# First batch of a two-layer transformer kernel: routing gates computed head by head inside the main loop, keys and queries with staging tiles of their own

## The chip, the cores and the metric

The kernel runs on one core of a Trainium2 chip. Its time is the device time of one execution in microseconds (us). The engines of the core are TensorE (PE; its weight loads are listed apart as PEld), VectorE (DVE), ScalarE (ACT), GpSimd (POOL) and SyncE (SP), which here only issues DMAs. Each engine runs its own instructions in the order in which they are written; engines wait for each other on semaphores alone.

## The reference

Input x has B = 4 batches of T = 1024 tokens with D = 128 features. Layer 0, which the change touches, is

```python
xn = layernorm(x)
x = x + multi_query_attention(xn)          # 16 heads of width 8, one key/value head
      + switch_head(xn)                     # 8 heads of width 128, 8 experts each
# switch_head: routing gates for values (gate_v) and for outputs (gate_o)
raw  = sigmoid(xn @ sel_w.T)                # [B, T, 8 heads, 8 experts]
vals, idx = top_k(raw, 2)                   # the two best experts of each head
gate = one_hot(idx) * vals / sum(vals) * route_scale
v    = sum over experts of gate_v * (xn @ v_w[h, e])
ctx  = softmax(q k^T * SCALE) v
out  = sum over experts of gate_o * (ctx @ o_w[h, e])
```

Layer 1 (a linear-feature attention and a routed feed-forward block) follows in the same launch and is not touched.

## The kernel before, in words

Layer 0 is a loop of software-pipelined steps. A step n (0 to 31) is one head h = n % 8 of one batch b = n // 8, of both attentions at once. Loop iteration i (from -2 to 34) on each engine is a list written out by hand: it ends step i, does most of step i + 1 and begins step i + 2. On DVE that is, for step i + 2, `split_queries` (two instructions over 128x1024), `take_peaks` (32 row maxima), `gate_values` (16 products of a PSUM tile with a gate), and for the steps before it `find_largest`, `join_largest`, `lower_ctx`, `output_gates`, `gate_outputs` and `lower_y`. TensorE writes all results but the sums into a ring of 7 PSUM tiles; a tile is claimed again when DVE or ACT has emptied it, in the order of claims.

Between these calls stand eight places, `batch_work(i, 0)` to `batch_work(i, 7)`, where work for another batch is slipped in. On DVE, place 0 stands before `join_largest(i + 1, 2)` and `split_queries(i + 2)`; place 1 between `split_queries` and `lower_ctx(i, 3)`; place 2 between `gate_values(i + 2, 1, 0)` and `(1, 1)`; place 3 within the peaks of tile row 4; place 4 before `gate_values(i + 2, 4, 1)`; place 5 before `lower_y(i + 2, 0)`; place 6 between `gate_values(i + 2, 5, 0)` and `(5, 1)`; place 7 before the last four peaks. In them batches 1 to 3 get their gates: iterations with i % 8 from 1 to 5 compute the gates of the batch after, one instruction or a few at each place.

Gates for four token tiles are made by `gates(b, part)`, 17 parts with 21 DVE instructions, each waiting for the one before it (`Chain`). Fifteen of them run over 128x512 elements, the others over 128x128 or 128x64. A batch takes two such passes.

Batch 0 has no loop to hide in; it is prepared ahead of the loop:

- SP loads x, 13 constants, the first weights, the rest of x, then stores zeros to two DRAM buffers `q_dram` (L747, L748), then stores the queries of each half (`store_queries`, three DMAs each, L669), then loads the queries of head 0 (`load_queries(0)`, four DMAs, L681), which waits until all stores have landed.
- PE turns xn, then computes `logits` (L419), then for each half `keys` (L427) and `queries` (L435), then `qk_products`.
- ACT waits for the constants, takes the root of the variance, keeps xnT, then `upper_x`, `upper_wv`, the four `sigmoid_exps`, then for each half `keep_keys` and `keep_queries`. Keys and queries of both halves go through one staging tile, `kf`, so each write waits until DVE (`lower_keys`) or the store's DMAs have read what was there.
- DVE takes the four `keep_v32`, `lower_keys(0, 0)`, the first pass of gates, `lower_keys(0, 1)`, `lower_qk`, the second pass of gates, and enters the loop with `split_queries(0)`.
- POOL lowers x (L87), adds a bias (L793) and lowers the first value weights (L87).

These lines are the preparation on DVE:

```python
for l in range(4):
    keep_v32(0, l)
lower_keys(0, 0)
for part in range(17):
    gates(0, part)
lower_keys(0, 1)
lower_qk()
for part in range(17, 34):
    gates(0, part)
```

Of the kernel before, what the change touches and what calls it, by code (L numbers as in the profile page):

```python
# [16 lines left out]
P = 128  # L17
# [162 lines left out]
def layer0(nc, whole, a, x, xnT, ident, order, combine, choice, xn_dram, listed, xs, spare, wvs, w):  # L180
# [4 lines left out]
    with ExitStack() as ctx:  # L185
# [15 lines left out]
        xo = oT[:, :].rearrange("p (t d) -> p t d", t=TPB)  # L201
        lg = m.sbuf("lg", [P, TPB, EM])
# [17 lines left out]
        probT = [m.sbuf(f"probT{k}", [P, TPB, 2 * P]) for k in range(2)]  # L220
        ctxT = [m.sbuf(f"ctxT{k}", [PS, 2, 2 * P]) for k in range(2)]
# [33 lines left out]
        steps, batches = range(N0), range(B)  # L255

# [9 lines left out]
        with nc.Block() as block:  # L266
            @block.tensor
            def _(pe):
# [378 lines left out]
            def _(sp):  # L647
# [13 lines left out]
                def store_queries(b, q):  # L661
# [5 lines left out]
                    for part in range(3):  # L667
                        rows = slice(2 + part * HD, 2 + (part + 1) * HD)
                        sp.dma_start(q_dram[b % 2][:, rows, q * 512:(q + 1) * 512], kf[:, :]).then_inc(q_stored, 16)  # L669
# [61 lines left out]
                def load_layer1():  # L731
                    sp.wait_ge(xn_turned, 2 * B)
                    sp.wait_ge(gates_ready, 2 * B)
# [158 lines left out]
            def _(act):  # L892
# [38 lines left out]
                def keep_turned(n, t, h):  # L931
# [95 lines left out]
                def keep_keys(b, q):  # L1027
# [7 lines left out]
                    if b or q:  # L1035
                        act.wait_ge(ks_ready, 2 * b + q)
                        act.wait_ge(q_stored, 64 + (96 * b if b else 48 * q))
                    act.activation(kf[:, :], ring.home["keys", b, q][:, :], ACT.Identity, bias=bk[:, :]).then_inc(k_kept, 1)

                def keep_queries(b, q):  # L1040
# [5 lines left out]
                    act.wait_ge(ks_ready, 2 * (b + 1) if b else q + 1)  # L1046
                    if b or q:
                        act.wait_ge(q_stored, 64 + 48 * (2 * b + q))
                    act.activation(kf[:, :], ring.home["queries", b, q][:, :], ACT.Identity, bias=bq[:, :], scale=HD ** -0.5)\
# [52 lines left out]
                keep_qk()  # L1102
# [89 lines left out]
            def _(v):  # L1192
# [20 lines left out]
                def gate_values(n, t, c):  # L1213
# [3 lines left out]
                    if t == 0 and c == 0:  # L1217
                        v.wait_ge(gates_ready, 2 * (n // HS + 1))
# [87 lines left out]
                ln, gs, mx = Chain(v, ln_step), Chain(v, gate_step), Chain(v, mix_step)  # L1306
# [47 lines left out]
                def lower_keys(b, q):  # L1354
                    if b not in batches:
# [3 lines left out]
                    v.scalar_tensor_tensor(out=kq.bitcast(F32R), in0=kq, scalar=split[:, 1:2], in1=kf[:, :],  # L1359
                                           op0=ALU.mult, op1=ALU.add).then_inc(ks_ready, 1)  # L1360

                def gates(b, part):
# [4 lines left out]
                    ranks = order[:, :].unsqueeze(1).to_broadcast([P, 64, ES])  # L1367
                    if part == 0:
                        v.wait_ge(gates_exp, 4 * b + 2 * q + 2)
                        gs(v.scalar_tensor_tensor(out=g_v[:, :, :], in0=flat, scalar=1.0, in1=flat, op0=ALU.add, op1=ALU.max))  # L1370
                    if part == 1:
                        gs(v.tensor_reduce(g_pair[:, 0, :], g_v[:, :, :], AX.X, ALU.min))
                    if part == 2:
                        gs(v.tensor_tensor(g_c[:, :, :], g_v[:, :, :], spread(g_pair[:, 0, :], ES), ALU.is_equal))
                    if part in (3, 9):
                        gs(v.tensor_tensor(g_c[:, :, :], g_c[:, :, :], ranks, ALU.mult))
# [1320 lines left out]
```

## Time and profile before

| | |
|---|---|
| time, median of 3 (lowest to highest) | 3180.81 us (3178.78 to 3181.18) |
| the profiled execution, its own time | 3167.05 us |
| its span, first to last instruction | 3165.2 us |
| mean granted TensorE clock | 0.969 |
| PE busy | 2945.3 us (93%) |
| DVE busy | 2427.8 us (77%) |
| POOL busy | 1846.8 us (58%) |
| ACT busy | 1619.2 us (51%) |

Busy times are sums over one execution. A step of the loop takes about 75 to 80 us; the preparation and the first two iterations take longer than the steady steps and use TensorE little. Durations below are those of the profiled execution, which is 13.8 us shorter than the median of the three runs.

### The profile page before, as it was taken

How to read it: one execution, taken by the hardware profiler on the slowest of the kernel's cores; microseconds unless marked ns; L12 is line 12 of the kernel's file. 1: busy time of each engine (PE TensorE's matmuls, PEld its weight loads, DVE VectorE, ACT ScalarE, POOL GpSimd, SP SyncE). 2: the span in 40 equal slices, each digit the busy share in tenths (PEclk: the TensorE clock that was granted, in tenths of full speed). 3: DMA queues.
4: the chain of work that ended last, by engine and by line, in shares of the span. 5: the costliest groups of instructions: out<-in, count | busy, mean ns of one | idle time of the engine just before them, and what ended most of it. 6: DMA issues, size and time to landing. Idle time of an engine off the chain costs nothing. (4 is left out here: it accounts for less than half of the span.)

```text
span 3165.2 us, 51840 instructions
## 1 busy us (share of the span) xinstructions
PE 2945.3 (93%) x17486; PEld 2054.4 (65%) x17486; DVE 2427.8 (77%) x4551; ACT 1619.2 (51%) x3277; POOL 1846.8 (58%) x2277
## 2 busy tenths in 40 slices
PE   4999999999999999999999999999999965798997
PEld 2666666666676666666666666666676643466674
DVE  7788898888889988898898988888888652245343
ACT  1455555555555555555555555555555621444634
POOL 2556666666676666666666676666666535334330
PEclk7999999999999999999999999999999978899998
DMA  5000001100100110101001100010010021133222
GB/s 168 21 22 22 22 22 32 32 22 23 37 27 22 32 32 22 29 23 36 29 22 32 32 22 23 22 43 28 22 39 22 10 43 45 56 89 110 84 76 85
DMA packets 139849, 124.63 MB, mean 39 GB/s; under 512 B 28410, under 2 KB 122116, under 8 KB 139492
## 3 DMA queue, kind: packets, MB, share of 16 engines
q1 hardware_dynamic: 125892, 88.46, 10.0%
q0 software_dynamic: 10160, 30.17, 3.0%
q10 hardware_dynamic: 3536, 2.69, 0.5%
q8 instruction: 143, 2.34, 0.3%
q14 instruction: 118, 0.97, 0.1%
HBM read 97.49 MB, written 29.30 MB: 40 GB/s over the span
## 5 line engine op out<-in xcount | busy, mean ns | idle before, releaser
L849 POOL TENSOR_TENSOR m_vprod<-m_vprod 128x512 f32<-128x512 f32 x256 | 336.1, 1313 | 721.4 <-DVE m_vprod L1223 721.4
L1210 DVE TENSOR_REDUCE m_peaks<-m_ring 128x1 f32<-128x512 f32 x1024 | 643.4, 682 | 23.9 <-PE m_ring L293 22.7
L957 ACT ACTIVATE m_expA<-m_ring 128x512 f32<-128x512 f32 x1024 | 543.9, 605 | 162.4 <-PE m_ring L366 159.2
L928 ACT ACTIVATE m_prob<-m_ring,m_negs 128x512 f32<-128x512 f32 x512 | 347.4, 684 | 404.4 <-DVE m_negs L1261 403.6
L344 PE MATMUL m_ring<-m_probT,m_vs 128*128 128x256 f32 x2048 | 473.8, 384 | 11.7 <-DVE m_oprod L1294 10.2
L344 PEld LDWEIGHTS m_ring<-m_probT,m_vs 128*128 128x128 f32 x2048 | 379.9, 190 | 83.8 <-issue 35.1
L1294 DVE TENSOR_TENSOR m_oprod<-m_ring,m_go 128x512 f32<-128x512 f32 x512 | 347.4, 685 | 73.5 <-POOL k_x L862 44.8
L1223 DVE TENSOR_TENSOR m_vprod<-m_ring,m_gate 128x512 f32<-128x512 f32 x512 | 348.8, 685 | 68.2 <-PE m_ring L99 41.0
L1251 DVE TENSOR_REDUCE m_negs<-m_ring 128x1 f32<-128x512 f32 x512 | 346.0, 685 | 39.2 <-PE m_ring L99 37.0
L858 POOL TENSOR_TENSOR m_oprod<-m_oprod 128x512 f32<-128x512 f32 x256 | 327.9, 1281 | 70.6 <-DVE m_oprod L1294 70.4
L938 ACT ACTIVATE m_probT<-m_ring 128x512 f32<-128x512 f32 x512 | 301.0, 605 | 103.9 <-PE m_ring L332 98.3
L332 PE MATMUL m_ring<-k_ident,m_prob 128*128 128x128 f32 x2048 | 309.6, 276 | 0.5 <-ACT m_probT L938 0.4
L332 PEld LDWEIGHTS m_ring<-k_ident,m_prob 128*128 128x128 f32 x2048 | 242.8, 141 | 76.0 <-issue 31.6
L381 PE MATMUL m_sums<-m_expA,m_v 128*32 128x512 f32 x2048 | 273.6, 606 | 0.6 <-ACT m_expA L957 0.5
L97 PE MATMUL m_ring<-k_wvs,k_xs 128*128 128x512 f32 (+1 forms) x536 | 234.3, 437 | 14.7 <-POOL k_wvs L87 7.0
L97 PE MATMUL m_ring<-k_xs,m_yT 128*128 128x512 f32 x512 | 219.8, 429 | 2.5 <-DVE m_oprod L1294 2.1
L97 PE MATMUL m_ring<-m_wos,m_ctxT 128*128 128x512 f32 x512 | 213.0, 416 | 1.0
L99 PE MATMUL m_ring<-k_wvs,k_xs 128*128 128x512 f32 (+1 forms) x536 | 212.3, 396 | 0.0
L98 PE MATMUL m_ring<-k_wvs,k_xs 128*128 128x512 f32 (+1 forms) x536 | 211.6, 395 | 0.0
L98 PE MATMUL m_ring<-m_wos,m_ctxT 128*128 128x512 f32 x512 | 202.9, 396 | 0.0
L99 PE MATMUL m_ring<-k_xs,m_yT 128*128 128x512 f32 x512 | 202.7, 396 | 0.0
L850 POOL TENSOR_TENSOR m_vprod<-m_vprod 128x256 f32<-128x256 f32 x256 | 190.8, 745 | 20.1
(311 smaller groups left out, 5396.9 us busy)
## 6 DMA issues: line engine op xcount, KB each, us to landing
m_wraw<-in_v_w SPq DMA_DIRECT2D x32, 512.0 KB, 4.0
m_qf<-q_dram SPq DMA_DIRECT2D x128, 128.0 KB, 2.7
m_wraw<-in_o_w SPq DMA_DIRECT2D x32, 512.0 KB, 4.0
q_dram<-m_kf SPq DMA_DIRECT2D x24, 256.0 KB, 3.0
listed<-in_pad SPq DMA_DIRECT2D x6, 897.0 KB, 12.2
m_xg<-listed SPq DMA_DIRECT2D x39, 138.0 KB
m_rows<-answers SPq DMA_DIRECT2D x8, 512.0 KB, 4.0
sums_dram<-m_sumsT ACTq DMA_DIRECT2D x128, 18.0 KB
```

What stands on the lines that cost most here:

```text
L97: pe.matmul(out, wh, xh, start=True, stop=False)
L98: pe.matmul(out, wh, xl, start=False, stop=False)
L99: return pe.matmul(out, wl, xh, start=False, stop=True)
L332: last = pe.transpose(ps[:, c * P:(c + 1) * P], prob[t % 2][:, (4 * h + c) * P:(4 * h + c + 1) * P], ident[:, :])
L344: last = pe.matmul(ps[:, 0:2 * P], vs[n % 2][:, k, :], probT[g % 2][:, k, :], start=(k == 0), stop=(k == TPB - 1))
L849: vchain(pool.tensor_tensor(vprod[:, 0:512], vprod[:, 0:512], vprod[:, 512:1024], ALU.add))
L928: act.activation(prob[t % 2][:, c * 512:(c + 1) * 512], ring.home["scores", n, t, c][:, :], ACT.Exp, bias=neg[t % 2], accum_out=den[n % 2] ...
L957: act.activation(expA[hh][:, c * 512:(c + 1) * 512], ring.home["scT", n, k, hh, c][:, :], ACT.Exp)\
L1210: v.tensor_reduce(peaks[:, t, hh, c:c + 1], ring.home["peaks", n, t, hh, c][:, :], AX.X, ALU.max)\
L1223: v.tensor_tensor(vprod[:, c * 512:(c + 1) * 512].rearrange("p (e d) -> p e d", e=4), ring.home["values", n, t, c][:, :].rearrange("p (e d ...
L1251: v.tensor_reduce(half_neg[:, t % 2, c:c + 1], ring.home["scores", n, t, c][:, :], AX.X, ALU.max, negate=True)\
L1294: v.tensor_tensor(oprod[t % 2][:, c * 512:(c + 1) * 512].rearrange("p (e d) -> p e d", e=4), ring.home["outputs", n, t, c][:, :].rearrange ...
```

## The change

The gates of batch 0 are made by `first_gates(h, part)`: one head at a time, for all eight token tiles, with the same 21 instructions in 17 parts as before, now over 128x128 elements (16 groups of 8 experts) where they ran over 128x512. Head 0 is done ahead of the loop. Head i + 3 is done in iteration i, so heads 1 to 7 in iterations -2 to 4: two parts at each of the places 0 to 6 and three at place 7. The scratch tiles lie in `oT`, which is first used later. All four exponentials of batch 0 are awaited before the first part.

The keys and queries of batch 0 get four staging areas in `probT[0]`, so the waits between them fall away; the first `keep_turned` takes up the wait for `ks_ready` and `q_stored` instead. PE and ACT do keys and queries before the logits; ACT takes the root before it waits for the constants, and does `upper_x` and `upper_wv` after the exponentials; DVE does both `lower_keys` first. No DMA is added, removed or moved in its queue.

```diff
+        h_v, h_one, h_c, h_other = (oT[:, k * P:(k + 1) * P].rearrange("p (g e) -> p g e", e=ES) for k in range(4))
+        h_pair, h_inv = (oT[:, k:k + 4 * TPB].rearrange("p (k g) -> p k g", k=2) for k in (4 * P, 4 * P + 4 * TPB))
+        h_m = oT[:, 4 * P + 8 * TPB:4 * P + 10 * TPB]
+        first_kf = probT[0][:, :, :].rearrange("p t q -> p (t q)").rearrange("p (w q d) -> p w q d", w=2, q=2)
+        def kf_of(b, what, q):
+            return kf[:, :] if b else first_kf[:, what, q, :]
...
# PE
-                for l in range(4):
-                    logits(0, l)
                 for q in range(2):
                     keys(0, q)
                     queries(0, q)
+                for l in range(4):
+                    logits(0, l)
...
# ACT, keep_turned
+                    elif g == 0 and t == 0 and h == 0:
+                        act.wait_ge(ks_ready, 2)
+                        act.wait_ge(q_stored, 64 + 96)
# ACT, keep_keys and keep_queries: the waits on ks_ready and q_stored only if b > 0, kf_of(b, ...) for kf
...
+                roots(1, slice(0, TPB))
                 act.wait_ge(consts_loaded, 16 * n_consts)
-                roots(1, slice(0, TPB))
                 keep_xnT(0, 0)
                 keep_xnT(0, 1)
-                upper_x(0)
-                upper_wv(0, ahead=True)
-                for l in range(4):
-                    sigmoid_exps(0, l)
                 for q in range(2):
                     keep_keys(0, q)
                     keep_queries(0, q)
+                for l in range(4):
+                    sigmoid_exps(0, l)
+                upper_x(0)
+                upper_wv(0, ahead=True)
                 keep_qk()
...
# DVE, gate_values
-                    if t == 0 and c == 0:
-                        v.wait_ge(gates_ready, 2 * (n // HS + 1))
# DVE: gate_part(chain, part, flat, tiles, n) holds the 21 instructions for both gates() and
+                def first_gates(h, part):
+                    if not 0 <= h < HS:
+                        return
+                    flat = gate_of[0][:, :, :].rearrange("p t (k g e) -> p (t k) g e", k=2, e=ES)[:, :, h, :]
+                    if part == 0:
+                        v.wait_ge(gates_exp, 4)
+                    gate_part(gs, part, flat, (h_v, h_one, h_c, h_other, h_m, h_pair, h_inv), 2 * TPB)
+                    if part == 16:
+                        gates_kept(v.tensor_tensor(flat, h_one, h_other, ALU.add))
...
                 def batch_work(i, place):
+                    for part in range(2 * place, 2 * place + 2 + place // 7):
+                        first_gates(i + 3, part)
                     if i not in steps:
                         return
...
+                lower_keys(0, 0)
+                lower_keys(0, 1)
                 for l in range(4):
                     keep_v32(0, l)
-                lower_keys(0, 0)
                 for part in range(17):
-                    gates(0, part)
-                lower_keys(0, 1)
+                    first_gates(0, part)
                 lower_qk()
-                for part in range(17, 34):
-                    gates(0, part)
```

## Rows read from the trace of the kernel before

**Rows 1.** The page, busy time of each engine: us, share of the span, instructions.
```profile
PE 2945.3 (93%) x17486; PEld 2054.4 (65%) x17486; DVE 2427.8 (77%) x4551; ACT 1619.2 (51%) x3277; POOL 1846.8 (58%) x2277
```

**Rows 2.** Timeline of the preparation: start, us, engine, line, tiles, [idle before <-releaser].
```profile
10.03 0.21 ACT L980 ACTIVATE m_rstd<-m_va 128x8 f32<-128x8 f32 x1 [1.33 <-DMA m_bq<-in_bq]
...
14.22 4.30 PE L419 MATMUL m_ring<-m_selv,k_xnT 128*128 128x160 f32 x16
...
18.76 0.85 SPq L748 DMA_DIRECT2D q_dram<-m_vprod  x1
...
19.21 1.02 PE L435 MATMUL m_ring<-k_xnT,m_wq 128*128 128x512 f32 x2
...
22.61 17.17 SPq L669 DMA_DIRECT2D q_dram<-m_kf  x6
...
27.01 0.69 ACT L1038 ACTIVATE m_kf<-m_ring,m_bk 128x512 f32<-128x512 f32 x1 [3.85 <-DMA q_dram<-m_kf]
...
37.27 0.69 ACT L1049 ACTIVATE m_kf<-m_ring,m_bq 128x512 f32<-128x512 f32 x1 [9.57 <-DVE m_ks L1359]
...
42.21 1.75 SPq L681 DMA_DIRECT2D m_qf<-q_dram  x4
...
55.16 0.80 PE L293 MATMUL m_ring<-m_ks,m_qs 32*128 32x512 f32 x4 [31.42 <-DVE m_qs L1202]
```

**Rows 3.** Timeline of DVE, instructions of the two passes of gates.
```profile
21.71 1.22 DVE L1370 SCALAR_TENSOR_TENSOR k_spare<-m_gate 128x512 f32<-128x512 f32 x1
...
39.68 0.68 DVE L1370 SCALAR_TENSOR_TENSOR k_spare<-m_gate 128x512 f32<-128x512 f32 x1
...
48.36 0.95 DVE L1391 RECIPROCAL m_g_inv<-m_g_pair 128x128 f32<-128x128 f32 x1
49.34 0.23 DVE L1392 TENSOR_TENSOR m_g_m<-m_g_inv 128x64 f32<-128x64 f32 x1
...
50.71 0.29 DVE L1398 TENSOR_TENSOR m_g_inv<-m_g_inv,m_g_m 128x128 f32<-128x128 f32 x1
```

**Rows 4.** Timeline of POOL, the first value weights lowered.
```profile
21.32 4.01 POOL L87 TENSOR_TENSOR k_wvs<-m_wraw,k_wvs 128x256 fp32r<-128x256 f32 x4
```

**Rows 5.** The page's DMA issues: count, KB each, us from issue to landing.
```profile
m_qf<-q_dram SPq DMA_DIRECT2D x128, 128.0 KB, 2.7
```

**Rows 6.** Waits of DVE from 55.1 to 95.6 us (iteration -2): total us, times, longest.
```profile
DVE m_vprod L1223 <- POOL m_vs L851: 8.2, 4, 2.8
```

**Rows 7.** Windows, one per step, iterations -1 to 6 and 15: length, busy us (x), PEclk, DMA share, GB/s.
```profile
95.64:166.97 71.33, 68.06 (x362) 46.23 (x363) 57.03 (x107) 39.37 (x85) 36.10 (x46) 0.95 0.08 23
166.97:255.85 88.88, 81.79 (x424) 55.45 (x422) 77.61 (x171) 45.53 (x94) 48.98 (x66) 0.94 0.07 19
255.85:333.53 77.68, 76.17 (x423) 52.94 (x422) 66.12 (x123) 44.90 (x94) 52.52 (x66) 1.00 0.08 22
333.53:410.99 77.46, 76.69 (x425) 53.12 (x424) 69.73 (x125) 43.43 (x93) 52.18 (x65) 1.00 0.08 22
410.99:488.76 77.77, 76.89 (x419) 52.44 (x418) 70.78 (x127) 43.39 (x92) 52.20 (x66) 1.00 0.08 23
488.76:565.13 76.37, 75.58 (x417) 52.03 (x416) 68.12 (x122) 43.10 (x91) 51.62 (x65) 1.00 0.12 33
565.13:641.19 76.06, 75.12 (x416) 51.82 (x414) 68.99 (x125) 41.64 (x89) 52.90 (x65) 1.00 0.12 33
641.19:715.79 74.60, 73.97 (x416) 51.32 (x414) 62.36 (x114) 41.67 (x89) 49.64 (x65) 1.00 0.09 23
...
1327.35:1401.99 74.64, 74.01 (x416) 51.36 (x414) 67.40 (x130) 41.67 (x89) 49.73 (x65) 1.00 0.08 24
```

**Rows 8.** Windows, one stretch around the turn from iteration 2 to 3.
```profile
400.95:424.96 24.01, 23.59 (x133) 17.36 (x134) 23.40 (x43) 15.48 (x34) 18.28 (x23) 1.00 0.07 23
```

**Rows 9.** Lines of DVE from 255.85 to 641.19 us: xcount, busy us, mean ns.
```profile
L1387 DVE TENSOR_TENSOR k_spare<-k_spare,m_g_pair 128x512 f32<-128x512 f32 x2 | 2.5, 1270 | 0.0
...
L1374 DVE TENSOR_TENSOR k_spare<-k_spare,m_g_pair 128x512 f32<-128x512 f32 x2 | 1.8, 894 | 0.0
```

More of the change, by code:

```diff
@@ L1034, in keep_keys @@
                                    ACT.Identity, bias=bk[:, :])
-                    if b or q:
+                    if b:
                         act.wait_ge(ks_ready, 2 * b + q)
-                        act.wait_ge(q_stored, 64 + (96 * b if b else 48 * q))
-                    act.activation(kf[:, :], ring.home["keys", b, q][:, :], ACT.Identity, bias=bk[:, :]).then_inc(k_kept, 1)
+                        act.wait_ge(q_stored, 64 + 96 * b)
+                    act.activation(kf_of(b, 0, q), ring.home["keys", b, q][:, :], ACT.Identity, bias=bk[:, :]).then_inc(k_kept, 1)
                 def keep_queries(b, q):
@@ L1045, in keep_queries @@
                     act.wait_ge(q_made, 2 * b + q + 1)
-                    act.wait_ge(ks_ready, 2 * (b + 1) if b else q + 1)
-                    if b or q:
+                    if b:
+                        act.wait_ge(ks_ready, 2 * (b + 1))
                         act.wait_ge(q_stored, 64 + 48 * (2 * b + q))
-                    act.activation(kf[:, :], ring.home["queries", b, q][:, :], ACT.Identity, bias=bq[:, :], scale=HD ** -0.5)\
+                    act.activation(kf_of(b, 1, q), ring.home["queries", b, q][:, :], ACT.Identity, bias=bq[:, :], scale=HD ** -0.5)\
                         .then_inc(q_kept, 1)
@@ L1358, in lower_keys, with gate_part @@
                     v.wait_ge(k_kept, 2 * b + q + 1)
-                    v.scalar_tensor_tensor(out=kq.bitcast(F32R), in0=kq, scalar=split[:, 1:2], in1=kf[:, :],
+                    v.scalar_tensor_tensor(out=kq.bitcast(F32R), in0=kq, scalar=split[:, 1:2], in1=kf_of(b, 0, q),
                                            op0=ALU.mult, op1=ALU.add).then_inc(ks_ready, 1)
+                def gate_part(chain, part, flat, tiles, n):
+                    vals, one, c, other, mo, pair, inv = tiles
+                    ranks = order[:, :].unsqueeze(1).to_broadcast([P, n, ES])
+                    if part == 0:
+                        chain(v.scalar_tensor_tensor(out=vals, in0=flat, scalar=1.0, in1=flat, op0=ALU.add, op1=ALU.max))
+                    if part == 1:
+                        chain(v.tensor_reduce(pair[:, 0, :], vals, AX.X, ALU.min))
+                    if part == 2:
+                        chain(v.tensor_tensor(c, vals, spread(pair[:, 0, :], ES), ALU.is_equal))
+                    if part in (3, 9):
+                        chain(v.tensor_tensor(c, c, ranks, ALU.mult))
+                    if part in (4, 10):
+                        chain(v.tensor_reduce(mo, c, AX.X, ALU.max))
+                    if part == 5:
+                        chain(v.tensor_tensor(one, c, spread(mo, ES), ALU.is_equal))
+                    if part == 6:
+                        chain(v.scalar_tensor_tensor(out=vals, in0=one, scalar=3.0e38, in1=vals, op0=ALU.mult, op1=ALU.add))
+                    if part == 7:
+                        chain(v.tensor_reduce(pair[:, 1, :], vals, AX.X, ALU.min))
+                    if part == 8:
+                        chain(v.tensor_tensor(c, vals, spread(pair[:, 1, :], ES), ALU.is_equal))
+                    if part == 11:
+                        chain(v.tensor_tensor(other, c, spread(mo, ES), ALU.is_equal))
+                    if part == 12:
+                        chain(v.reciprocal(inv, pair))
+                        chain(v.tensor_tensor(mo, inv[:, 0, :], inv[:, 1, :], ALU.add))
+                    if part == 13:
+                        chain(v.tensor_tensor(mo, mo, tiny[:, :].to_broadcast([P, n]), ALU.max))
+                        chain(v.reciprocal(mo, mo))
+                        chain(v.tensor_tensor(mo, mo, route[:, :].to_broadcast([P, n]), ALU.mult))
+                    if part == 14:
+                        chain(v.tensor_tensor(inv, inv, mo.unsqueeze(1).to_broadcast([P, 2, n]), ALU.mult))
+                    if part == 15:
+                        v.tensor_tensor(one, one, spread(inv[:, 0, :], ES), ALU.mult)
+                        chain(v.tensor_tensor(other, other, spread(inv[:, 1, :], ES), ALU.mult))
```

45 lines of the change are left out of this document (6 added, 39 removed).

## The prediction

> **What bounds the kernel now.** I read the page first, then the windows by step, then the timeline of the preparation engine by engine. The page shows TensorE busy for 93% of the span [rows 1]; a change in DVE work pays or costs only where TensorE waits for it. The windows show where that is. In a step with little extra work (iteration 6) TensorE is busy 73.97 of 74.60 us while DVE has 12.2 us to spare; in iterations 2 to 4 DVE's spare time is down to 7.7, 7.0 and 8.3 us [rows 7]. The timeline of the preparation shows the opposite: the first matmul of the loop starts at 55.16 us after TensorE has stood idle for 31.42 us, released by `split_queries` on DVE (L1202) [rows 2]. There DVE is what counts. Behind it lies a chain through one staging tile: ACT waited 3.85 us for the stores of the first queries, then 9.57 us for `lower_keys(0, 1)`, which stood behind the first pass of gates; only then could the second half be stored (loads issued at 42.21 us), and the second pass of gates held DVE until 53 us anyway [rows 2].
>
> So the change takes DVE work from a place where all of it is on the path, and puts most of it, in smaller pieces, into steps that are bound by TensorE but have DVE nearly full.
>
> **What one head costs on DVE.** An instruction over 512 elements takes 0.68 us, over 128 elements 0.29, over 64 elements 0.23; a reciprocal over 128 takes 0.95 [rows 3]. From one start to the next it is some 0.035 us more. Of the 21 instructions of a head 15 run over 128 elements: 15 x 0.325 = 4.9 us. The reciprocals over 32 and 16 elements and the four others come to an estimated 1.5 us. A head alone is 6.4 us, eight heads 51 us. The two passes before took 14.7 and 13.4 us (21.7 to 36.4, 39.7 to 53.1), 28 us. The change adds 23 us of DVE work, because the fixed part of an instruction is paid four times as often.
>
> The Trainium skill speaks against this edit (VectorE: DVE Perf Modes, section on the TRN2 errata): a fixed latency is paid per instruction, so tiles should have 512 elements or more. The rows above agree, a quarter of the elements costs 0.29 of 0.68 us; by elements alone the eight heads would cost 28 us.
>
> POOL adds to this. With POOL lowering weights from 21.32 on [rows 4], the first gate instruction took 1.22 us, the same one later 0.68 [rows 3]; in iterations 1 to 5 the same kind averaged 0.89 and 1.27 us on two lines [rows 9]. So an instruction with two SBUF operands waits 0 to 0.6 us for POOL. I take 0.26, near the lower of the two lines, for the 12 large instructions of that kind: 3.1 us, 9.5 us for a head in the loop. That this wait is as long for a short instruction as for a long one is my choice; if it goes by length it is 1.2 us, if there is none a head is 6.4.
> The Trainium skill would choose the same (SBUF — State Buffer, section on the two sides of SBUF): it calls the port pair of VectorE and GpSimd an exclusive lock held for a whole instruction.
>
> **The preparation, step by step.** (1) The root no longer waits for the last constant: 1.33 us less [rows 2]. (2) xnT is complete at 13.7 us; four matmuls of keys and queries, at 0.86 us each, end at 16.3, the logits (4.3 us for all) at 20.5 [rows 2]. (3) ACT's six evictions end at 17.6; table load, exponentials after the last logits: 21.4. (4) Stores: SP has issued the zero fills by 19.61 [rows 2]; nothing of this moves. Six stores at 0.6 us are issued by 23.3. Before, three issued at 22.61 had landed at 27.0, and the other three took 4.2 us from 38.0 to 42.21 [rows 2]. All six landed: 25.7 (23.3 + 2.4) to 31.2 (27.0 + 4.2); I take 28.8, one more trio of data behind the first. (5) The four loads issue over 1.75 us, the last 1.3 after the first, and land 2.7 later [rows 2, 5]: 32.9, between 29.7 and 35.2. (6) DVE: gates of head 0 from 21.4, 6.4 + 3.1 us beside POOL, to 30.9; `lower_qk` 1.3; place 0 of iteration -2 0.7: 32.9. Both arrive together. `split_queries` takes 2.0: first peak matmul at 35.0 instead of 55.16, **20 us earlier** (17 to 22). POOL's lowering moves from 25.3 to 31.4 at the latest, still before the first values. ACT's `upper_x` and `upper_wv` stand before `keep_qk`, hidden behind the gates. The new wait in `keep_turned` holds ACT's queue for nothing: keys and stores are 50 us old then. The dropped wait of `gate_values` and the one at the end of a head cost nothing, DVE's own order covers them. SP's wait in `load_layer1` counts the same event.
>
> **What is given back in the loop.**
> - Iteration -2 is a chain of DVE and POOL: DVE waits 8.2 us for POOL in four waits [rows 6]. The parts at places 2, 3, 4 and 6 lie on it (0.65 each) and the three at place 7 (1.15); place 5 falls in a wait, place 1 in the wait for the first peaks. 3.75 us, with POOL's waits 4.3 (up to 5.5).
> - Iterations -1 to 4 get 9.5 us each. Two bounds. *Saturation:* iterations 6 and 15 differ by 5.0 us of DVE work and not in length, iteration 5 has 6.6 more than 6 and is 1.46 longer [rows 7]; as if DVE could be busy 90% for nothing and each us beyond cost 0.9. *Filling:* the 24 us around the turn from iteration 2 to 3 had DVE busy 23.40 us and TensorE 23.59 [rows 8], so DVE can be full without stopping TensorE; then only what does not fit beside 2 us of idle time counts.
> - Iterations 2, 3, 4: filling 69.7 + 9.5 + 2 - 77.5 = 3.7, likewise 4.5 and 3.2, sum 11.4; saturation 3 x 8.5 = 25.6. Iteration 1: 0 or 5.0. Iteration 0: 0.2 or 6.2. Iteration -1: 0.65 (place 0 stands before a `split_queries` that TensorE awaits) or 1.9 [rows 7].
> - Sum with iteration -2: 16.0 (with 3.75) by filling, 44 by saturation. I take a third of the way, **25.5 us**, since the stretch of rows 8 is direct evidence and the parts are small and spread.
>
> What is late next: a late DVE empties ring tiles late, and TensorE stops at a claim. From iteration 7 on nothing differs.
>
> **Sum.** -20 + 25.5 = +5.5 us: 3172.6 us for an execution like the profiled one (3167.05), 3186.3 against the median of the runs, which stands 13.8 us above that execution.
>
> **Rivals.**
> - *Filling, B.* -20 + 16 = -4: 3176.8 us. For it: rows 8. Against it: no step in rows 7 shows DVE above 91% with gates in it.
> - *The steps swallow it, D, the other side.* Short instructions don't wait for POOL, a head costs 6.4 us and the idle time of the steps takes it: filling gives 0.6 + 1.4 + 0.1 = 2.1 in iterations 2 to 4, 0.65 and 3.75 before: 6.5 in all, -13.5: 3167.3 us. It decides if the loop gives back less than 12.6 us. For it: iterations 6 and 15.
> - *Saturation, C.* Each us on DVE is paid: -20 + 44 = +24: 3204.8. For it: iterations 3 and 5. It may bring the clock down as in iterations -1 and 0 (0.95 and 0.94) [rows 7].
> - *A short preparation gain, E.* Each of the 12 instructions of head 0 waits 0.54 us for POOL as the first one did (1.22 against 0.68), or loads land at 35.2: 17 us gained, 3189.3. The lock rule of the Trainium skill (SBUF — State Buffer, the section on the two sides) works this way: whoever comes second waits for the whole instruction. The trace agrees for the first instruction and leaves the short ones open.
> - That the change does not do what it says is excluded by the order of the queues: nothing else holds the second stores.
>
> **Chances.** Forecast A 0.35 (its own range 3180 to 3193), B 0.25, D 0.18, C 0.14, E 0.08. Below 0.2% (6.4 us) a difference can't be told from none here. Faster: D and a fifth of B, 0.23. Slower: C, most of E, over half of A, 0.39. The rest 0.38. The forecast stands at the edge of "slower"; what is likely is a small number either way. Range: from between D and B, 3171, to just short of C, 3200.
>
> **What would show it.** In the profile after: first L293 matmul at 34 to 38 us, released by L1202; the DMA loads of m_qf issued at 27 to 31 us; no idle of 9 us on ACT; `cut_peaks(0)` (L1233, at 93.25 before) 15 to 16 us earlier; iterations 2 to 4 longer by 3 to 8 us each with DVE above 95% busy; the 128x128 gate instructions at 0.29 us alone and with a mean of 0.5 beside POOL; from iteration 7 on the same lengths. The prediction is wrong if these iterations keep their length (then D), or if the queries land after 35 us.

## The result

The changed kernel takes 3206.46 us (median of 4, 3202.74 to 3208.58) where the kernel before, run beside it, takes 3179.80 (4 runs, 3175.00 to 3181.18): ratio 1.0102, interval 1.0083 to 1.0122. It is 1% slower; the two medians by themselves are 26.7 us apart. The forecast was 3186.3 with a range of 3171 to 3200, so the prediction was wrong. The rival *Saturation*, 3204.8, came nearest.

The profiled execution took 3206.8 us (span 3205.0, mean granted clock 0.965), 39.8 us more than the profiled one of before. At the start of iteration 30, the last mark that is compared here, it is 35.3 us behind (2512.72 and 2477.39). The other 4.4 us lie behind that mark, nearly all of it layer 1. That rest varied between the profiled executions of all kernels here: 654 to 661 us in the four that were taken on one chip, 688 to 705 in the ten others, with no order by kernel. So the traces are compared up to that mark, and times by the ratios of one comparison.

**The page**, busy time of each engine [rows 1]:

```profile
PE 2973.6 (93%) x17486; PEld 2070.6 (65%) x17486; DVE 2473.6 (77%) x4677; ACT 1619.9 (51%) x3277; POOL 1849.0 (58%) x2277
```

DVE has 126 instructions and 45.8 us more. PE has 28.3 us more busy time for the same instructions; why is told with the clock, below.

**The preparation**, from the timelines of the changed kernel [rows 2]:

```profile
16.32 0.71 ACT L1060 ACTIVATE m_probT<-m_ring,m_bq 128x512 f32<-128x512 f32 x1
17.04 1.28 ACT L1034 ACT_TABLE_LOAD   x1
...
19.58 0.29 DVE L1376 SCALAR_TENSOR_TENSOR m_oT<-m_gate 128x128 f32<-128x128 f32 x1 [1.16 <-ACT m_gate L1034]
...
19.97 5.26 SPq L677 DMA_DIRECT2D q_dram<-m_probT  x6
...
21.20 2.00 DVE L1386 TENSOR_TENSOR m_oT<-m_oT 128x128 f32<-128x128 f32 x1
...
28.07 1.75 SPq L689 DMA_DIRECT2D m_qf<-q_dram  x4
...
32.21 0.69 DVE L83 CAST m_qs<-m_qf 128x1024 fp32r<-128x1024 f32 x1 [0.16 <-DMA m_qf<-q_dram]
...
34.28 0.80 PE L301 MATMUL m_ring<-m_ks,m_qs 32*128 32x512 f32 x4 [14.34 <-DVE m_qs L1213]
```

The first peak matmul starts at 34.28 us instead of 55.16: 20.9 us earlier, 20 were forecast. The chain is the one forecast. The queries are kept at 17.0, the six stores follow without the long waits of before, the loads go out at 28.07, and DVE waits for them 0.16 us only, since its gates of head 0 end at 30.2. One of those, 0.29 us long by itself, was held for 2.00 us while POOL lowered x.

**The loop**, one window for each iteration from -2 to 6 [rows 7]. The first window begins with the first peak matmul, each later one where TensorE starts the transposes of `qf` for the next head. Columns are length, busy us (x) of PE, PEld, DVE, ACT, POOL, then PEclk, DMA share, GB/s:

```profile
34.28:80.61 46.33, 36.12 (x93) 20.41 (x93) 38.69 (x71) 1.19 (x2) 16.89 (x21) 0.68 0.29 101
80.61:155.76 75.15, 68.80 (x361) 46.55 (x362) 66.21 (x128) 39.41 (x85) 37.02 (x47) 0.95 0.08 22
155.76:252.49 96.73, 83.38 (x424) 56.36 (x423) 83.78 (x192) 45.56 (x94) 49.51 (x66) 0.93 0.06 18
252.49:338.77 86.28, 80.66 (x423) 54.93 (x422) 75.57 (x144) 45.09 (x94) 52.75 (x66) 0.96 0.07 20
338.77:425.20 86.43, 81.95 (x425) 56.10 (x424) 78.75 (x146) 43.44 (x93) 51.73 (x65) 0.96 0.07 20
425.20:511.62 86.42, 82.05 (x419) 55.31 (x418) 79.20 (x148) 43.59 (x92) 52.05 (x66) 0.96 0.07 20
511.62:598.01 86.39, 80.19 (x418) 54.63 (x416) 77.59 (x143) 43.06 (x91) 51.26 (x65) 0.96 0.10 29
598.01:674.84 76.83, 75.69 (x415) 52.00 (x414) 69.67 (x125) 41.60 (x89) 52.32 (x64) 1.00 0.11 33
674.84:749.49 74.65, 73.94 (x416) 51.35 (x415) 62.40 (x114) 41.67 (x89) 49.77 (x65) 1.00 0.09 23
```

Set against rows 7 (iteration -2 of before is the 40.48 us from 55.16 to 95.64, with DVE busy 31.40), all in us:

| iteration | longer by | forecast (filling / saturation) | DVE busy, added | DVE idle, before | DVE idle, after |
|---|---|---|---|---|---|
| -2 | 5.9 | 3.75 to 5.5 | 7.3 | 9.1 | 7.6 |
| -1 | 3.8 | 0.65 / 1.9 | 9.2 | 14.3 | 8.9 |
| 0 | 7.9 | 0.2 / 6.2 | 6.2 | 11.3 | 13.0 |
| 1 | 8.6 | 0 / 5.0 | 9.5 | 11.6 | 10.7 |
| 2 | 9.0 | 3.7 / 8.5 | 9.0 | 7.7 | 7.7 |
| 3 | 8.7 | 4.5 / 8.5 | 8.4 | 7.0 | 7.2 |
| 4 | 10.0 | 3.2 / 8.5 | 9.5 | 8.3 | 8.8 |

Look at the last two columns. In iterations 2 to 4 DVE is given 9 us of work and has about as much idle time as before: in sum, none of it was filled. The seven iterations give back 53.8 us; 25.5 were forecast and 44 was the upper bound. Iteration 5 adds 0.8; nearly all later ones agree to some tenths. -20.9 + 53.8 is +32.9; iteration 5 and small differences of the 24 later ones make it the 35.3 us at the mark.

**What DVE waits for.** Its longer waits in iteration 3 (total us, times, longest), before:

```profile
DVE m_ctxT L87 <- ACT m_ctxT L948: 2.0, 3, 1.3
DVE m_oprod L1294 <- POOL k_x L862: 1.4, 1, 1.4
```

and in the changed kernel:

```profile
DVE m_vprod L1232 <- PE m_ring L99: 1.6, 3, 0.6
DVE m_oprod L1303 <- POOL k_x L870: 1.4, 1, 1.4
DVE m_negs L1260 <- PE m_ring L99: 1.4, 3, 0.7
```

The wait for ACT shrank from 2.0 to 0.4 us, so the new work did fill that one. The waits for TensorE grew from 2.2 us in all to 4.0, and the one for POOL stayed at 1.4. The rows read as an exchange: DVE comes late, TensorE stops, and later DVE waits for what TensorE has not made. Iteration 1 shows the same, 4.7 to 1.7 us for ACT and 4.9 to 6.8 for TensorE.

**What TensorE sees.** Four neighbouring windows in iteration 3 of the changed kernel:

```profile
432.11:435.57 3.46, 3.40 (x18) 2.77 (x16) 3.35 (x6) 2.75 (x7) 3.30 (x4) 1.00 0.00 0
435.57:439.02 3.45, 1.95 (x15) 0.58 (x15) 3.31 (x6) 2.05 (x4) 2.74 (x4) 1.00 0.01 2
439.02:442.48 3.46, 3.45 (x9) 2.22 (x10) 2.85 (x5) 1.09 (x2) 0.00 (x0) 0.58 0.54 152
442.48:445.94 3.46, 3.46 (x17) 2.78 (x16) 2.40 (x5) 1.09 (x2) 1.96 (x2) 0.92 0.00 0
```

DVE is full (3.31 of 3.45) and TensorE stands idle for 1.5 us; 0.6 us after it works again, its granted clock goes to the lower of its two levels, 1.2 GHz of 2.4, for 3.4 us. The waits of PE in this iteration name the places:

```profile
PE m_ring L374 <- DVE m_ctxT L87: 1.5, 1, 1.5
PE m_ring L374 <- ACT m_prob L936: 1.1, 1, 1.1
PE m_ring L301 <- DVE m_oprod L1303: 0.7, 1, 0.7
```

Before, the longest wait of this iteration was 0.4 us and its clock was 1.00. Now each of iterations 1 to 4 spends 8% of its length at half clock (PEclk 0.96): 0.04 x 86.4 = 3.5 us of full-clock time is lost in each, 14 of the 19.5 us by which PE's busy time grows in these four. Whether that makes the iterations longer is a question of its own, and kernels 10 and 11 ask it.

### The profile page after: what moved, and what is told of

It is laid out like the page before. It is cut to its first block and busy times, and to the rows that moved or that the text cites. A ratio compares the mean times of both kernels' runs of the same rounds, so it can differ in the third digit from the quotient of the medians.

```text
span 3205.0 us, 51986 instructions
## 1 busy us (share of the span) xinstructions
PE 2973.6 (93%) x17486; PEld 2070.6 (65%) x17486; DVE 2473.6 (77%) x4677; ACT 1619.9 (51%) x3277; POOL 1849.0 (58%) x2277
## 5 line engine op out<-in xcount | busy, mean ns | idle before, releaser
L352 PE MATMUL m_ring<-m_probT,m_vs 128*128 128x256 f32 x2048 | 475.5, 385 | 12.2 <-DVE m_oprod L1303 10.6
L97 PE MATMUL m_ring<-k_wvs,k_xs 128*128 128x512 f32 (+1 forms) x536 | 236.8, 442 | 13.0 <-POOL k_wvs L87 6.0
L99 PE MATMUL m_ring<-k_wvs,k_xs 128*128 128x512 f32 (+1 forms) x536 | 215.1, 401 | 0.0
L98 PE MATMUL m_ring<-k_wvs,k_xs 128*128 128x512 f32 (+1 forms) x536 | 214.4, 400 | 0.0
L374 PEld LDWEIGHTS m_ring<-m_qs,m_ks 32*128 32x128 f32 x1024 | 64.0, 182 | 229.7 <-issue 119.5
```

What stands on the lines that cost most here:

```text
L97: pe.matmul(out, wh, xh, start=True, stop=False)
L98: pe.matmul(out, wh, xl, start=False, stop=False)
L99: return pe.matmul(out, wl, xh, start=False, stop=True)
L352: last = pe.matmul(ps[:, 0:2 * P], vs[n % 2][:, k, :], probT[g % 2][:, k, :], start=(k == 0), stop=(k == TPB - 1))
```

## The experiments

Every kernel of a comparison ran on one chip beside the kernel before. In the first comparison that one took 3133.83 us, in the others 3181.37, 3181.76 and 3181.21: chips differ by more than the change, so only ratios are used. An unchanged copy, profiled on the chip of the first comparison, agrees with the first profile of before within 1.6 us at the start of iteration 30.

**1. The preparation alone.** Heads 1 to 7 get no gates:

```diff
                 def batch_work(i, place):
-                    for part in range(2 * place, 2 * place + 2 + place // 7):
-                        first_gates(i + 3, part)
```

> The changed kernel with the gates of heads 1 to 7 of batch 0 left out altogether (their exponentials are used as gates), so only the preparation is changed. All theories: the first peak matmul of the loop at 34.3 us as in the changed kernel (55.2 before), and all iterations as long as before. Time 3159 us, ratio 0.9935 (21 us less). If the ratio is above 0.997, the early start is lost again later without any gate work, and the loop is not where the loss lies.

Measured: ratio 0.9942 (0.9921 to 0.9963), some 18 us less (15 by the medians alone); at the start of iteration 30 it is 21 us ahead of the unchanged copy on the same chip. The first peak matmul starts at 34.40 us and every iteration keeps its length of before (40.46, 71.24, 88.71, 77.66, 77.59, 77.75, 76.38). The gain ahead of the loop is real and lasts, and what the changed kernel loses it loses to the pieces in the loop.

**2. The same number of instructions, half of them without a second SBUF operand.** 10 of the 21 instructions of heads 1 to 7 become row maxima over the same 128x128 elements, so these heads get no valid gates:

```diff
                 def first_gates(h, part):
...
+                    if h and part in (2, 3, 5, 6, 8, 9, 11, 15, 16):
+                        for k in range(1 + (part == 15)):
+                            (gates_kept if part == 16 else gs)(v.tensor_reduce(h_m, h_v, AX.X, ALU.max))
+                        return
```

> The changed kernel, but for heads 1 to 7 ten of the 21 instructions, those over 128x128 with two SBUF operands, are row maxima over the same 128x128 elements instead (0.28 us each, one operand; the gates of these heads are not made). The number of instructions stays. Theory saturation by busy time: DVE work falls by what was waited for POOL, about 3 us a head, and so does each step: iterations 1 to 4 go from 86.4 to 83 us, time about 3188, ratio 1.002. Theory that number and place of the instructions count and not their length: no change, 3205. Theory filling: with 6.3 us a head the work fits in, iterations 1 to 4 at 79 us, time 3173.

Measured: ratio 1.0038 (1.0024 to 1.0052). In iterations 1 to 4 DVE's busy time grows by 6.3, 5.7, 4.9 and 6.3 us and the lengths by 6.2, 4.7, 4.1 and 6.0. Iteration 3:

```profile
412.62:494.45 81.83, 78.04 (x419) 52.81 (x418) 75.68 (x148) 43.60 (x92) 51.66 (x66) 1.00 0.08 22
```

The same number of instructions gives back 21.0 us in these iterations instead of 36.2: it is their time on DVE that counts. DVE idles 6.2 us of iteration 3.

**3. Where the pieces stand.** All 17 parts at places 2 to 7, none at the turn from one iteration to the next (before `split_queries` and `lower_ctx`):

```diff
-                    for part in range(2 * place, 2 * place + 2 + place // 7):
-                        first_gates(i + 3, part)
+                    if place >= 2:
+                        for part in range(3 * place - 6, min(3 * place - 3, 17)):
+                            first_gates(i + 3, part)
```

> The changed kernel with the same 21 instructions per head, but none at places 0 and 1 (before split_queries and lower_ctx): three parts at each of places 2 to 6, two at place 7. Theory saturation: the same DVE work in the same iteration, the same time, 3206 us, ratio 1.008 to 1.012. Theory turn: TensorE stops at the turn of an iteration because split_queries and lower_ctx come late, and its clock falls to half after it; with places 0 and 1 free iterations 1 to 4 fall from 86.4 to 81 us or less with the clock at 1.00, time 3185 or less, ratio 1.002.

Measured: ratio 1.0083 (1.0060 to 1.0106); iterations 1 to 4 at 84.8, 83.2, 84.3 and 82.7 us with 8.4, 7.3, 7.1 and 8.3 us more on DVE. They give back 25.8 us instead of 36.2, and half of that difference is that the same instructions waited less for POOL (31.1 us of DVE time added instead of 36.4). The place is worth some 5 us in these four; as the main cause the turn is ruled out. Iteration 4 is 6.4 us longer here though its clock stays at 1.00.

**4 and 5. DVE work that nobody needs, put into the kernel before**, where the gates of batch 0 don't disturb: 16 instructions over 128x128 in each of iterations 5 to 9, two at each place. In the fourth kernel they are row maxima, in the fifth products of two SBUF tiles:

```diff
+                    for _ in range(2 if 5 <= i <= 9 else 0):
+                        extra(v.tensor_reduce(ex_m, ex_a, AX.X, ALU.max))         # 4
+                        extra(v.tensor_tensor(ex_b, ex_b, ex_a, ALU.mult))        # 5, instead
```

> The kernel before (gates of batch 0 ahead of the loop as before), with extra work alone: in iterations 5 to 9 two row maxima over 128x128 elements, each waiting for the one before, at each of the eight places: 16 x 0.31 = 5.0 us more DVE work per iteration, one operand each, nothing waits for them. Before, these iterations have DVE busy 69.0, 62.4, 66.2, 63.6 and 65.6 us and last 76.1, 74.6, 74.6, 75.5 and 76.0. Theory ceiling at 90 to 91% busy: iteration 6 (67.4 of 74.6) keeps its length, 7 (71.2) becomes 78.5, 8 and 9 (68.6, 70.6) 75.5 and 78, iteration 5 (74.0) 81.5. Theory that every us costs from the first on: all five 4 to 5 us longer. Theory filling: none longer by over 0.5 us but iteration 5.

> As the run with extra row maxima, but the 80 extra instructions multiply two SBUF tiles of 128x128 elements. Alone such an instruction takes 0.29 us too. Theory that the wait for POOL does not depend on the length of the instruction: a mean of 0.55 us or more, single ones above 1.5 us, DVE busy some 4 us more per iteration than with the row maxima, and iterations longer by about 0.9 of that. Theory that the wait goes by length, as 1.06 to 0.69 for 512 elements: a mean of 0.35 us and iterations as long as with the row maxima within 1 us.

Measured, one run each: 3186.08 and 3199.48 us, beside 3181.37 of before. Lines of DVE over the two kernels, first 4, then 5:

```profile
L1496 DVE TENSOR_REDUCE m_oT<-m_oT 128x16 f32<-128x128 f32 x80 | 22.4, 280 | 1.4
```

```profile
L1496 DVE TENSOR_TENSOR m_oT<-m_oT 128x128 f32<-128x128 f32 x80 | 46.6, 582 | 1.4
```

A product that takes 0.29 us alone [rows 3] takes 0.58 in the loop, a row maximum 0.28: the second operand costs 0.29 us on average. It is the wait for POOL: the 28 products that started while POOL was idle took 0.28 us on average and never over 0.30, the 52 that started while POOL was busy 0.74. The price of DVE time (us):

| iteration | DVE idle before | 4: DVE added, longer by | idle left | 5: DVE added, longer by | idle left |
|---|---|---|---|---|---|
| 5 | 7.1 | 4.7, 3.8 | 6.1 | 8.2, 7.8 | 6.7 |
| 6 | 12.2 | 3.7, 0.3 | 8.9 | 8.8, 1.4 | 4.9 |
| 7 | 8.4 | 4.2, 2.4 | 6.7 | 7.7, 4.3 | 5.0 |
| 8 | 11.9 | 3.6, 0.2 | 8.5 | 8.2, 1.8 | 5.5 |
| 9 | 10.4 | 5.7, 1.1 | 5.8 | 9.0, 4.2 | 5.6 |

Here the threshold is seen directly. Between 8 and 9 us cost 1.4 us in iteration 6, which had 12.2 us to spare, and 7.8 in iteration 5, which had 7.1. Whatever an iteration had, 5 to 7 us of DVE's idle time are left when it is full. Iterations 5 and 6 of the fifth kernel:

```profile
567.10:650.97 83.87, 79.61 (x416) 54.05 (x415) 77.16 (x143) 41.66 (x89) 52.74 (x65) 0.98 0.10 30
650.97:726.95 75.98, 75.41 (x415) 51.90 (x414) 71.13 (x130) 41.82 (x89) 49.96 (x65) 1.00 0.08 23
```

**6. The new staging and order with both wide passes ahead**, nothing in the loop:

```diff
-                for part in range(17):
-                    first_gates(0, part)
+                for part in range(34):
+                    gates(0, part)
```

> The changed preparation (staging tiles, order, root), but both passes of gates over 128x512 elements are made ahead of the loop as in the kernel before, and none in the loop. Theory that the start is bound by DVE once the staging waits are gone: gates from 19.6 us, 28 us of them and 3 us of waits for POOL, lower_qk 1.3, split_queries 2: first peak matmul at 53 to 55 us against 55.2, ratio 0.999 to 1.000. Theory that the staging chain was the bound and gates were in its shadow: 40 us, ratio 0.995.

Measured: ratio 0.9998 (0.9989 to 1.0007). The first peak matmul starts at 53.57 us. The new staging and order alone are worth 1.6 us: with the chain of stores gone, the 28 us of gates on DVE set the start.

**7. Fewer iterations, wider instructions**, the gates complete: head 0 ahead, head 1 in iteration -2, heads 2 and 3 at once (256 wide) in -1, heads 4 to 7 at once (512 wide) over iterations 0 and 1:

```diff
+                    if i < -1:
+                        todo, heads = range(2 * place, 2 * place + 2 + place // 7), slice(1, 2)
+                    elif i < 0:
+                        todo, heads = range(2 * place, 2 * place + 2 + place // 7), slice(2, 4)
+                    elif i < 2:
+                        todo, heads = range(8 * i + place, 8 * i + place + 1 + i * (place // 7)), slice(4, 8)
...
```

> The same gates complete, but the heads are taken in wider instructions: head 0 ahead, head 1 in iteration -2, heads 2 and 3 by one 256-wide pass in iteration -1, heads 4 to 7 by one 512-wide pass over iterations 0 and 1, nothing in iterations 2 to 4. Ceiling theory: the DVE time beyond the free 4 us is paid in iterations 0 and 1 alone: -20.9 us ahead, +5.5 in iteration -2, +5 to 6 in -1, +7 to 8 in each of 0 and 1: +5 to +6 us in all, ratio 1.001 to 1.003, iterations 2 to 4 at their 77.5 us again. Per-instruction theory (each two-operand instruction beside POOL costs the same wait, so that the number of instructions and not their length decides): iterations 0 and 1 cost 4 us or less each, total -3 us or better, ratio 0.999 or less.

Measured: ratio 1.0012 (1.0002 to 1.0022). Iterations -2 to 1 are longer by 5.9, 5.4, 4.6 and 9.2 us, iterations 2 to 4 as before, which is what the ceiling gives in sum (the split between 0 and 1 was expected even). But iterations 0 and 1 paid 4.6 us for 5.3 us of DVE time and 9.2 for 9.4, though each had over 11 us idle before: next to nothing was free there. A price by the instruction is ruled out: 13 more of them in iteration 1 cost 9.2 us, as much as 21 short ones did, because they are longer.

**8. Pieces only where DVE has room**, the gates complete: heads 0 and 1 ahead (256 wide), heads 2 to 7 in one pass 768 wide over iterations -2 and -1:

```diff
+                    at = {-2: (0, 0, 1, 2, 3, 4, 5, 6, 7), -1: (7, 7, 7, 9, 11, 13, 14, 15, 17)}.get(i)
+                    for part in range(*at[place:place + 2]) if at else ():
+                        first_gates(slice(2, 8), part)
...
-                    first_gates(0, part)
+                    first_gates(slice(0, 2), part)
```

> The changed preparation with gates of heads 0 and 1 ahead in one pass over 128x256 elements, and heads 2 to 7 in one pass over 128x768 elements in iterations -2 and -1 (none at place 0): 42 instructions instead of 168, and none in iterations 0 to 4, where DVE is near its ceiling. Theory ceiling: first matmul at 37 to 38 us, iteration -2 longer by 5 to 6, iteration -1 by 4 to 6, all others as before: 5 to 8 us less than before, ratio 0.9975 to 0.9985. If work in iterations -2 and -1 costs in full (22 us), ratio 1.001.

Measured: 3171.33 us against 3181.37, ratio 0.9969 (0.9957 to 0.9982): faster than both kernels. Iterations -2 to 1:

```profile
36.17:81.63 45.46, 36.47 (x92) 20.58 (x92) 37.91 (x59) 1.19 (x2) 17.40 (x21) 0.68 0.25 81
81.63:158.74 77.11, 70.54 (x361) 47.45 (x362) 69.49 (x121) 39.14 (x85) 38.45 (x47) 0.96 0.07 21
...
248.23:325.94 77.71, 76.20 (x424) 52.95 (x422) 66.17 (x123) 44.90 (x94) 52.57 (x66) 1.00 0.08 22
```

It gives back 5.0 and 5.8 us in the first two iterations, where DVE had 9.1 us of 40 and 14.3 of 71 idle and was given 6.5 and 12.5. Iteration 0 is 0.6 us longer, as it is by 0.4 in the unchanged copy, and nothing is given back after it.

**9. Edits 2 and 3 together** (heads 1 to 7 again without valid gates).

> The changed kernel with both earlier edits at once: of the gate instructions of heads 1 to 7, 10 of 21 are one-operand row maxima (so heads 1 to 7 get no valid gates), and the pieces stand at places 2 to 7 of an iteration alone. Ceiling theory (an iteration of about 77.7 us has some 4 us of DVE time to fill, and each us of DVE work beyond costs 0.8 to 1.0 us): DVE is given about 5 to 5.5 us in each of iterations 1 to 4, one more is saved by the places, so they come to 79 to 81 us instead of 86.4, layer 0 ends about 5 to 8 us earlier than with the one-operand edit alone, and the ratio to the kernel before is 0.999 to 1.002. Turn theory (work in the places beside the cores' turns is what costs): as the gates are off the turns already in the earlier run, the one-operand form adds little, iterations 82 to 84 us, ratio 1.005 or more.

Measured: ratio 1.0045 (1.0032 to 1.0058), between the two expectations. Iterations 1 to 4 are longer by 3.3, 3.9, 4.3 and 5.9 us for 6.7, 5.3, 5.1 and 6.3 us on DVE, so 0.5 to 0.9 us for each; iteration 0 is 96.07, 2.9 us longer than in kernel 2. The ceiling holds (idle left: 8.2, 6.3, 6.2, 7.9 us), but which places cost more than others in iteration 0 isn't settled.

**10 and 11. Is it the clock?** The changed kernel (10) and the kernel before (11) get six more 128x512 matmuls, overwritten at once, at each of six points of iterations 1 to 4. Four of the points, in iterations 2 and 3, stand where the changed kernel had a gap and then half clock. The one in iteration 1 comes at 268.14 us, when the clock has already fallen, and the one in iteration 4 fills a gap after which the clock had not fallen.

```diff
                 def scores_by_key(n, k, hh, c):
...
+                    if hh == 0 and c == 0 and (k, n) in ((0, 2), (0, 3), (0, 4), (6, 3), (6, 4), (6, 5)):
+                        for _ in range(2):
+                            matmul3(pe, ps[:, :], both(xs[b % 2], slice(0, P)), both(xs[b % 2], slice(0, 512)))
```

> The changed kernel, and TensorE does six more 128x512 matmuls (1.4 us at full clock, overwritten at once) at six points where it stood idle for 1.1 to 1.5 us and its granted clock then fell to half: before the scores of key tile 0 in steps 2, 3, 4 and of key tile 6 in steps 3, 4, 5. Clock theory (a full DVE makes gaps, the gaps bring the clock down, and the half clock costs 1.7 us at each fall, 3.4 us in each of iterations 1 to 4): the granted clock of these iterations goes from 0.96 to 0.98 or 1.00, and each is 1.5 to 3.4 us shorter, in all 6 to 12 us less than the changed kernel, ratio to the kernel before 1.006 to 1.008. Rival (DVE sets the length, the slow TensorE only uses up time in which it would wait): the clock may recover, but the iterations keep 86 to 87 us and the ratio 1.010. If the fillers themselves delay: 88 us.

> The kernel before with the same six groups of extra matmuls: the price of a filler where TensorE has no gap to fill. Both theories: 1.4 us each where nothing is idle, some 6 to 8 us in all, iterations 1 to 4 at 79 to 80.5 us with the clock at 1.00, ratio 1.002 to 1.003.

Measured: ratios 1.0110 (1.0092 to 1.0128) and 1.0029 (1.0016 to 1.0042). In kernel 11 iterations 1 to 4 are 79.20, 79.28, 79.00 and 77.62 us, 5.5 us more than in the unchanged copy for some 8.2 us of matmuls. In kernel 10 they are 88.76, 86.50, 87.98 and 86.87: 4.6 us more than in the changed kernel. Their clock is 0.94, 0.98, 0.96 and 0.96, so it rose in iteration 2 only, where the clock theory had 0.98 to 1.00 in all four; the rival's 86 to 87 us and 1.010 came nearer. Iteration 2 is the one to read. Timeline of PE in kernel 10 where the first filler stands (its weights are `k_xs` alone), and later, at the end of this iteration:

```profile
355.92 0.40 PE L99 MATMUL m_ring<-k_xs 128*128 128x512 f32 x1
356.25 0.72 PE L377 MATMUL m_ring<-m_qs,m_ks 32*128 32x512 f32 x4
...
357.48 0.40 PE L98 MATMUL m_ring<-k_wvs,k_xs 128*128 128x512 f32 x1
...
412.90 0.50 PE L301 MATMUL m_ring<-m_ks,m_qs 32*128 32x512 f32 x1
415.80 0.75 PE L301 MATMUL m_ring<-m_ks,m_qs 32*128 32x512 f32 x3 [2.40 <-DVE m_oprod L1306]
```

and the same places in the changed kernel:

```profile
353.34 1.00 PE L374 MATMUL m_ring<-m_qs,m_ks 32*128 32x512 f32 x3 [0.84 <-DVE m_ctxT L87]
...
355.10 0.63 PE L98 MATMUL m_ring<-k_wvs,k_xs 128*128 128x512 f32 x1
...
413.37 0.49 PE L301 MATMUL m_ring<-m_ks,m_qs 32*128 32x512 f32 x1
414.58 0.50 PE L301 MATMUL m_ring<-m_ks,m_qs 32*128 32x512 f32 x3 [0.72 <-DVE m_oprod L1303]
```

Here the filler does what it should: with the gap filled the next matmuls run at full clock, 0.40 us each where the changed kernel needs 0.63. So at this place the clock's fall hangs on the gap. A gap isn't always followed by one: after 2.61 us of idle time at 325.57 us the clock of the changed kernel stayed at 1.00. Counted from the start of the iteration (341.45 and 338.77), L301 is reached at 71.45 us instead of 74.60, over 3 us ahead. Then TensorE stands still for 2.40 us instead of 0.72, because DVE, which ran without a pause for 13 us up to there, had not come to `gate_outputs` (L1306). Just ahead of that product DVE had five gate instructions in a row, four of them of the first batch. Two of these, and the product:

```profile
412.00 1.36 DVE L1408 TENSOR_TENSOR m_oT<-m_oT 128x128 f32<-128x128 f32 x1
...
413.60 0.69 DVE L1431 TENSOR_TENSOR m_gate<-m_oT 128x128 f32<-128x128 f32 x1
...
415.05 0.69 DVE L1306 TENSOR_TENSOR m_oprod<-m_ring,m_go 128x512 f32<-128x512 f32 x1
```

The clock falls there instead, and the iteration ends at 86.50 us, as in the changed kernel at 86.43. Iteration 3 repeats it: its wait of 0.7 us at L301 becomes 2.4. In both, what the clock gave was taken back by the wait for DVE. Nor is a fall of the clock needed for the loss: the six iterations of kernels 2, 3 and 9 among 1 to 4 whose clock stayed at 1.00 are 3.3 to 6.4 us longer, 0.5 to 0.84 us for each us on DVE. The changed kernel paid 0.9 to 1.06. Part of that difference may be the clock's, which no run here shows. How much shorter the iteration would be with the clock held at full throughout can't be read from these runs, since the fillers cost time themselves.

## Why the prediction was wrong

**Right: the preparation.** 20.9 us for 20, by the forecast steps: loads issued at 28.07 (27 to 31 was said), no idle time of 9 us on ACT, start at 34.28 (34 to 38), released by `split_queries`. `cut_peaks(0)` came 15.0 us earlier (15 to 16). Two terms were off and nearly cancel, which is luck: head 0 took 10.6 us (19.6 to 30.2) where 9.5 was said, as one instruction took 2.00 and one 1.23 us beside POOL; and it began at 19.6 instead of 21.4. Most of that is the logits, which took 2.3 us (15.82 to 18.16) where 4.3 was carried over from before; why they are faster there isn't known. The root came 2.7 us earlier, not 1.33, but keys and queries ended only 0.3 us ahead of the forecast.

**Right in sum: a head's cost on DVE.** 9.5 us were said; iterations 1 to 4 got 9.5, 9.0, 8.4 and 9.5. Both terms were off, and they cancel: there are 11 large instructions with two operands, not 12, and they took 0.64 us on average, 0.36 more than alone and not 0.26; the rest of a head is shorter, since 6.4 us counted the pauses between instructions. Two products over 128x128 in the changed kernel, iterations 1 to 4:

```profile
L1405 DVE TENSOR_TENSOR m_oT<-m_oT 128x128 f32<-128x128 f32 x4 | 5.4, 1356 | 0.1
...
L1382 DVE TENSOR_TENSOR m_oT<-m_oT,k_order 128x128 f32<-128x128 f32 x8 | 4.0, 498 | 0.3
```

So the mean wait for POOL of a short instruction (0.36 us here, 0.29 in kernel 5) lies between those of the two long ones of rows 9 (0.2 and 0.6), as was chosen. By place it runs up to 1.1 us. The Trainium skill (SBUF — State Buffer, on the two sides of SBUF) calls the pair a lock held for a whole instruction, taken by a DVE instruction with two SBUF inputs against a GpSimd instruction that reads SBUF; kernels 4 and 5 agree, one operand 0.28 us, two 0.58.

**Right: fixed costs.** The 28 us of two wide passes became 10.6 us of head 0 and 59.0 us of DVE time in the loop. The Trainium skill (VectorE: DVE Perf Modes, TRN2 errata) spoke against narrow tiles for this reason. Kernel 7 agrees: the same seven heads in wider instructions added 33.4 us of DVE time in iterations -2 to 1 and none behind them.

**Wrong: "I take a third of the way, 25.5 us, since the stretch of rows 8 is direct evidence".** This is the step that failed. *Filling* took it that DVE can be filled up to 2 us of idle time in an iteration, from one stretch of 24 us in which it was full and TensorE too. The runs show 7 to 9 us left in iterations 2 to 4 of the changed kernel, and no less than 4.9 in any iteration of any kernel. The trace of before had said so: windows over its iterations -2 to 28 give DVE between 6.6 and 14.3 us of idle time, never less, though several hold a stretch like that of rows 8. A full stretch shows that DVE may run late for 24 us, not that an iteration can be full. Iterations 2 to 4 gave back 27.6 us: saturation said 25.6, filling 11.4, the forecast stood at some 16.

**Wrong too: the bounds of iterations 0 and 1.** 0.2 to 6.2 and 0 to 5.0 were said, 7.9 and 8.6 measured, above even saturation. I set the threshold by DVE's mean share (90%) and so gave iteration 1, with 11.6 us idle, 4 us for nothing. It isn't the mean alone: in iteration 1 DVE kept 10.7 us idle, in kernel 7 11.4, and in kernel 9, with the pieces elsewhere and cheaper, 8.2. Where the pieces fall against the waits counts for 2 to 3 us an iteration. Why iterations 0 and 1 kept so much more idle time than iterations 5 to 9 of kernel 5 stays open. Iteration -1 gave back 3.8 (said 0.65 to 1.9), iteration -2 5.9 (4.3, up to 5.5).

**The expected sign "DVE above 95% busy" was wrong.** It stays at 90 to 92% in iterations 2 to 4. DVE sets their length without being full, because it takes its work in one order and waits several times in each iteration for what TensorE, ACT or POOL make (some 6 us in all in iteration 3, before and after). The share itself is no fixed ceiling: iterations 6 and 7 of kernel 5 reach 94%.

**The clock** was named under *Saturation* and came: 0.96 in iterations 1 to 4.

In short, rival *Saturation* was the mechanism, at -20.9 + 53.8 instead of -20 + 44. That its 3204.8 lies within 2 us of the median is luck in part: its price of the loop was 10 us short, and the medians are 26.7 us apart where the two profiled executions are 39.8.

## What to carry to other kernels

Before work is moved from a prologue into a pipelined loop, give each engine its idle time per iteration and ask how low it has ever been seen: here DVE, in order and coupled to TensorE by a ring of tiles, never got below 4.9 us in 76, so an iteration with 7 us idle has next to nothing to give. One with 12 has some 7 at most: iteration 6 of kernel 5 had them, iterations 0 and 1 had 11 to 12 us idle and gave next to nothing in the changed kernel and in kernel 7. A short stretch in which both engines are full shows that an engine may run late for a while, not that it has room. Put the moved work into the iterations with the most idle time (one of the first two here: kernel 8, 10 us faster than before) and in wide instructions. Where TensorE's clock falls, look for the gap ahead of it and for the engine that it waits for there: filling such gaps with useless matmuls gained nothing as long as DVE was late.

## What the runs showed of the hardware

- After TensorE stood idle for 0.8 to 1.5 us within otherwise dense work, four times in iterations 2 and 3 of the changed kernel, its granted clock was at 1.2 GHz for 3.4 us, and matmuls over 128x512 took 0.63 us of modelled time instead of 0.39. With 1.4 us of otherwise useless matmuls in these gaps it stayed at 2.4 GHz there. It also stayed there after gaps of 2.61 us in iteration 1 and of 0.74 and 1.24 us at the start of iteration 4 of the changed kernel, so the length of a gap alone doesn't tell.
- A DVE product over 128x128 with two SBUF operands takes 0.29 us alone, 0.58 on average beside a POOL that is busy for two thirds of the time (0.28 when it starts while POOL is idle, 0.74 when POOL is busy), and up to 2.00 once; a row maximum over the same tile takes 0.28 in the same places.
- The same kernel took 3133.8 us on one chip and 3181.4 on another. Two profiled executions of it, 3135.4 and 3167.1 us, differ by 33.3 us behind the start of iteration 30, where layer 1 lies (654.6 and 687.9), and by 1.6 us before it.
